# The second layer's bias in a mixture-of-experts kernel: from 39 TensorE products to additions on VectorE, with the order of the work written anew

## The chip, the core and the metric

The kernel runs on one core of one Trainium2 chip. The metric is the device time of one execution in microseconds (us), with the median of several runs.

## The reference, cut to what matters

The input is x, of 2 x 2048 rows of 128 numbers. Each row is normalised; the normalised rows go through causal attention and, beside it, through a layer of eight experts (each row uses one); both results are added to x.

```python
xn = _layernorm(x)
# attention, per batch of 2048 rows
scores = einsum('bsd,de,bte->bst', xn, qk, xn) / SCALE      # causal mask, softmax over t
attn_out = einsum('bst,btd,de->bse', attn, xn, ov)
# experts: D = 128, F = 512, E = 8
eid   = argmax(xn @ centroids.T)                            # one expert for each row
alpha = sigmoid(sum(xn * centroids[eid]))
xln   = layernorm(xn) * ln_g[eid] + ln_b[eid]
h     = relu(xln @ w1[eid] + b1[eid])
y     = h @ w2[eid] + b2[eid]                               # the bias of this page is b2
out   = x + attn_out + (xn + alpha * y)
```

## The kernel before, in words

All five engines take their work from one hand-written list, ORDER (lines 68 to 131). A word such as `OUT.7` is a job with its arguments. Each engine walks through the whole list and carries out the jobs that are its own, in the list's order; semaphores connect the engines. So the list sets the order on every queue, and a job that waits holds up all that stands behind it on its engine.

Precision is got by splitting a number into a 16-bit high half and a 16-bit low half (`_hi`, `_lo`), and multiplying high by high, high by low and low by high.

The work falls into stages. The names are those of the jobs.

- Start: rows are loaded and normalised (VAR, LE, RN, ROW on VectorE and ScalarE, XA on ScalarE), turned (T), projected (Q, V), and the first matrices of the experts are folded with gain and bias (W1, then W1h and W1l for their halves; for experts 4 to 7 the low half W1l is VectorE's). W2 and W2l split the second matrices.
- Attention, steps 0 to 51 of 80: `M` computes a block of scores only for its row maxima, `MR` (VectorE) reduces it, `RM` joins the maxima, `SH` turns them, `SHa` (ScalarE) writes them into row 0 of the queries as the shift. Then for each step `X` (TensorE, three products) computes scores, `EH` and `EX` (ScalarE) their exponentials, `XL` (VectorE) the low half, `P` and `PB` (TensorE) the weighted sums, and `QT` (VectorE) divides.
- Routing: CH, PL, BLK and SIG on VectorE find each row's expert and its place. `SC` (GpSimd, 32 indirect transfers) scatters the rows sorted by expert, each with its weight alpha/256 and its row number behind it, into `sorted_x`. SyncE then reads them back, turned for TensorE (`turn_rows`) and plain (`load_rows`, into `xs`, which is the tile `xn`).
- Experts: 39 tiles of 128 sorted rows. `HI.k` (lines 1434 to 1436, 12 products of 128 columns) computes the hidden layer of tile k, `RE.k` (ScalarE, line 1165) its high half with the relu, `LO.k` (VectorE, line 1014) its low half, and `OUT.k` (lines 1454 to 1460, 13 products) the output. Three hidden tiles may be on their way at once (HB = 3). TensorE's order runs `HI` two or three tiles ahead of `OUT`. The first of the 13 products, line 1454, adds the bias: the stationary operand is `pick`, a matrix of the expert's one-hot column, the moving operand the high and low halves of b2 (`b2_hl`). `REG` loads the list of experts into TensorE's registers, 20 words with two experts each, and every operand of an expert is addressed through them.
- `YS.k` (ScalarE, line 1173) evicts two tiles of output from PSUM, scaled by each row's weight, into `xs`. `SO.t` (GpSimd, line 679, 39 indirect transfers) stores tile t by row number into `sorted_y`; it waits for the eviction of its pair (`s_ysb`).
- End: the last 28 steps of attention (52 to 79) run on TensorE, while SyncE loads `sorted_y` back (line 566, eight transfers, after all stores) and `Y` (VectorE, line 933) adds it to x; the rows go out as they are finished.

Three preparations serve the bias alone: two small transfers of b2, its split on ScalarE (line 1092) and VectorE (line 958), and the building of `pick` on ScalarE (line 1095, job PICK).

Of the kernel before, what the change touches and what calls it, by code (L numbers as in the profile page):

```python
# [72 lines left out]
Z.3 W1.2 M.0.0.0.0 M.0.0.2.0 M.0.0.3.0 M.0.0.1.0 W1b.1 W1b.2 V.1 T.2 M.0.1.0.1 M.0.1.2.0 W1.3 M.0.1.1.1 M.0.1.3.1 W1b.3
M.0.1.0.0 SH.0.0 M.0.1.3.0 Tl.2 MR.0.1.0.1 MR.0.1.2.0 MR.0.1.1.1 MR.0.1.3.1 MR.0.1.0.0 ROW.4.6 ROW.6.8 MR.0.1.3.0 R2
MR.0.1.1.0 MR.0.1.2.1 W1l.4 W1l.5 RM.0.1 Ql.2 MR.0.2.0.1 MR.0.2.2.1 MR.0.2.2.0 MR.0.2.3.2 MR.0.2.0.2 MR.0.2.3.1 W1h.2
XA.2 W1l.1 Vf.1 Ta.2 W1l.2 LE.4.6 LE.6.8 W1h.3 W2.0 W2.1 W1l.3 SHa.0.0 XA.3 W1h.4 W1h.5 Qa.2 EX.0 XA.5 EX.1 EX.2 SHa.0.1
R2a W1.4 W1.5 M.0.1.1.0 M.0.1.2.1 Q.2 X.0 X.1 X.2 M.0.2.0.1 M.0.2.2.1 P.0 M.0.2.2.0 SH.0.1 M.0.2.3.2 M.0.2.0.2 M.0.2.3.1
# [1416 lines left out]
```

## Time and profile before

| what | us |
|---|---|
| median of 3 runs (213.14 to 215.27) | 214.18 |
| the profiled execution, its time | 215.02 |
| the profiled execution, its span | 213.3 |
| TensorE busy in the span | 201.8 |
| VectorE busy in the span | 172.8 |
| ScalarE busy in the span | 159.2 |

The span runs from the first to the last instruction; the 1.72 us by which the execution's own time is longer lie around it. Times in the rows are us from the span's start. A busy TensorE is not one at its peak: a product of 128 columns is shown as 0.22 us long, while the next one starts 0.056 us after it.

### The profile page before, as it was taken

The page shows a single profiled execution, that of the slowest core. Times are in us where ns is not written, and L with a number is a line of the kernel's source. Part 1 is how long each engine was busy: PE and PEld are TensorE (multiplying, and loading weights), DVE is VectorE, ACT ScalarE, POOL GpSimd, SP SyncE. Part 2 cuts the span into 40 slices and gives each one's busy share as a digit, 9 for nine tenths or more (in the row PEclk, how much of TensorE's full clock was granted, in tenths as well). Part 3 has the DMA queues.
Part 4 walks back from the last instruction along what each step waited for, and adds up shares of the span by engine and source line. Part 5 has one row for each costly group of instructions (what it writes and reads, how often), then busy time and mean ns, then how long its engine had stood idle before and what let it go on. Part 6 is the DMA issues. An engine that isn't in the chain of part 4 may idle for free.

```text
span 213.3 us, 6804 instructions
## 1 busy us (share of the span) xinstructions
PE 201.8 (95%) x2404; PEld 157.2 (74%) x2404; DVE 172.8 (81%) x449; ACT 159.2 (75%) x370; POOL 112.7 (53%) x159
## 2 busy tenths in 40 slices
PE   7887798999999999999979999999999999999993
PEld 5644256779677856777648999999999987777782
DVE  5899998989999999999999857549376564559974
ACT  2689996899978898787886664655765568988881
POOL 7338557972618787776760256676355677300000
PEclk9999999999999999999999999999999999999998
DMA  5993004168112111111117856665771111194065
GB/s 171 302 292 112 2 0 153 51 219 268 50 52 82 47 52 53 50 50 53 50 33 151 149 127 151 141 138 77 157 165 38 52 52 55 49 292 130 0 194 155
DMA packets 37616, 23.54 MB, mean 110 GB/s; under 512 B 12488, under 2 KB 34160, under 8 KB 37584
## 3 DMA queue, kind: packets, MB, share of 16 engines
q1 hardware_dynamic: 34976, 18.28, 33.5%
q0 software_dynamic: 2272, 4.69, 6.7%
q8 instruction: 20, 0.33, 0.7%
q10 hardware_dynamic: 336, 0.14, 0.3%
q14 instruction: 12, 0.10, 0.2%
HBM read 11.17 MB, written 9.38 MB: 96 GB/s over the span
## 4 chain that ended last, share of the span: by engine, by line
PE 79%; ACT 5%; DVE 2%; issue 2%; DVEq 0%; ACTq 0%
PE psum L1298 6%; PE psum L1299 6%; PE psum L1297 6%; PE psum L1350 6%; PE psum L1342 6%; PE psum L1343 6%; PE psum L1276 6%; PE psum L1434 4%; PE psum L1460 4%; PE psum L1436 4%; PE psum L1435 4%; PE psum L1458 4%; PE psum L1459 4%; PE psum L1333 4%; ACT xn L1063 1%
## 5 line engine op out<-in xcount | busy, mean ns | idle before, releaser
L679 POOL DMA_INDIRECT sorted_y<-xn x39 | 38.2, 980 | 26.8 <-ACT xn L1173 14.3
L896 DVE TENSOR_TENSOR p_lo<-p_sb,p_hi 128x512 f16<-128x512 f32 (+1 forms) x68 | 42.3, 654 | 11.1 <-ACT p_sb L1046 10.9
L1040 ACT ACTIVATE p_hi<-psum 128x512 f16<-128x512 f32 (+1 forms) x68 | 35.9, 545 | 15.8 <-PE psum L1350 12.6
L1014 DVE SCALAR_TENSOR_TENSOR h_lo<-psum,h_hi 128x512 f16<-128x512 f32 x39 | 26.6, 690 | 21.3 <-ACT h_hi L1165 21.1
L671 POOL DMA_INDIRECT sorted_x<-xr,pos x32 | 33.1, 1034 | 15.4 <-issue 10.2
L1046 ACT ACTIVATE p_sb<-psum 128x512 f32<-128x512 f32 (+1 forms) x80 | 39.4, 544 | 0.1
L1165 ACT ACTIVATE h_hi<-psum 128x512 f16<-128x512 f32 x39 | 23.2, 599 | 17.9 <-PE psum L1436 16.9
L882 DVE TENSOR_REDUCE row_max<-psum 128x1 f32<-128x512 f32 x48 | 31.6, 682 | 0.7 <-PE psum L1276 0.5
L1342 PE MATMUL psum<-v_hi,p_hi 128*128 128x129 f16 x236 | 31.2, 221 | 0.0
L1343 PE MATMUL psum<-v_lo,p_hi 128*128 128x128 f16 x236 | 31.2, 219 | 0.0
L1276 PE MATMUL psum<-kT_hi,qT_hi 128*128 128x512 f16 (+3 forms) x80 | 26.0, 349 | 4.9 <-DVE row_max L878 1.9
L1458 PE MATMUL psum<-w_hl,h_hi 128*128 x156 | 28.1, 219 | 0.0
L1459 PE MATMUL psum<-w_hl,h_hi 128*128 x156 | 28.1, 219 | 0.0
L1460 PE MATMUL psum<-w_hl,h_lo 128*128 x156 | 28.1, 219 | 0.0
L1297 PE MATMUL psum<-qT_hi,kT_hi 128*128 128x512 f16 (+1 forms) x80 | 27.8, 347 | 0.0
L1298 PE MATMUL psum<-qT_lo,kT_hi 128*128 128x512 f16 (+1 forms) x80 | 27.8, 347 | 0.0
L1299 PE MATMUL psum<-qT_hi,kT_lo 128*128 128x512 f16 (+1 forms) x80 | 27.8, 347 | 0.0
L1434 PE MATMUL psum<-x2T,w_hl 128*128 128x128 f16 x156 | 27.5, 219 | 0.1
L1435 PE MATMUL psum<-x2T,w_hl 128*128 128x128 f16 x156 | 27.5, 219 | 0.0
L1436 PE MATMUL psum<-x2T,w_hl 128*128 128x128 f16 x156 | 27.5, 219 | 0.0
L1342 PEld LDWEIGHTS psum<-v_hi,p_hi 128*128 128x128 f16 x236 | 23.0, 98 | 2.2 <-DVE x_sb L923 0.5
L1343 PEld LDWEIGHTS psum<-v_lo,p_hi 128*128 128x128 f16 x236 | 23.1, 98 | 1.7
(190 smaller groups left out, 493.5 us busy)
## 6 DMA issues: line engine op xcount, KB each, us to landing
w_raw<-in_L_ffn_w SPq DMA_DIRECT2D x16, 256.0 KB, 5.0
sorted_x<-zero SPq DMA_DIRECT2D x3, 780.0 KB, 4.7
xn<-sorted_x SPq DMA_DIRECT2D x8, 260.0 KB, 4.1
x_sb<-in_L_attn_input_data SPq DMA_DIRECT2D x8, 256.0 KB, 5.7
xn<-sorted_y SPq DMA_DIRECT2D x8, 256.0 KB, 5.0
out<-x_sb SPq DMA_DIRECT2D x6, 256.0 KB, 3.1
sorted_y<-xn POOLq DMA_INDIRECT x39, 2.9
sorted_x<-xr,pos POOLq DMA_INDIRECT x32, 2.5
```

The costliest lines, as they stand in the source:

```text
L679: pool.indirect_dma_start(out=sorted_y[:, :], out_offset=bass.IndirectOffsetOnAxis(ap=tokens, axis=0), in_=xs[:, t % SLOTS, 0:P], in_offse ...
L896: v.tensor_tensor(p_lo[:, u, off:GW], p_sb[:, u, off:GW], p_hi[:, u, off:GW], ALU.subtract).then_inc(s_plo, 1)
L1046: a.activation(p_sb[:, u, off:GW], bank[SCORE[n % R]][:, off:GW], ACT.Exp, scale=SCALE).then_inc(s_exp, 1)
L1276: mm(at[:, 0:w], qT_hi[:, q:q + P], kT_hi[:, k:k + w], start=True, stop=True).then_inc(s_mm, 1)
L1297: mm(at[:, off:GW], kT_hi[:, kk], qT_hi[:, q], start=True, stop=False)
L1298: mm(at[:, off:GW], kT_hi[:, kk], qT_lo[:, q], start=False, stop=False)
L1299: m = mm(at[:, off:GW], kT_lo[:, kk], qT_hi[:, q], start=False, stop=not diag)
L1342: mm(to[i], w, v_hi[:, kt, 0:P + 1], start=(j == 0 and (i % 2 == 0 or (i == GT - 1 and (b, g) == LAST_QT[:2]))), stop=False, skip_group_ch ...
L1343: mm(to[i][:, 0:P], w, v_lo[:, kt, :], start=False, stop=False, skip_group_check=True)
L1458: mm(to, h_hi[:, h, at], hi, start=False, stop=False, skip_group_check=True)
L1459: mm(to, h_hi[:, h, at], lo, start=False, stop=False, skip_group_check=True)
L1460: m = mm(to, h_lo[:, h, at], hi, start=False, stop=(c == FC - 1), skip_group_check=True)
```

## The change

The product of line 1454 is gone, with `pick`, `b2_hl` and their preparation; the first product of a tile's first chunk now starts the accumulation. In their place

- SyncE loads b2 broadcast to all 128 partitions (job `B2`, 128 x 1024 numbers) into `A_e`, which the first matrices no longer need then. It waits until all eight of them are done;
- ScalarE scales that by 256 (job `B2s`, one instruction, between YS.0 and RE.5);
- VectorE loads the list of experts into its own registers (`REGv`, between LO.4 and LO.5) and, after each eviction YS.k, adds bias times weight to the evicted tiles (`YB.k`, one SCALAR_TENSOR_TENSOR for each of the two tiles, 39 in all, the bias addressed by register);
- GpSimd's stores wait for YB (`s_yb`) in place of YS.

ORDER is written anew throughout: the jobs other than these are the same, in another sequence.

```diff
 ORDER = entries("""
-... RE.0 RE.1 RE.2 RE.3 YS.0 RE.4 RE.5 RE.6 YS.1 YS.2 RE.7 ...
+... RE.0 Qa.7 RE.1 RE.2 RE.3 RE.4 YS.0 B2s RE.5 RE.6 RE.7 YS.1 YS.2 ...
...
-    N_FILL = 6
+    N_FILL = 5
...
-        w1_bytes, w2_bytes, pick_bytes = (flat(t[:]).bitcast(U8) for t in (w1_hl, w2_hl, pick))
+        w1_bytes, w2_bytes = (flat(t[:]).bitcast(U8) for t in (w1_hl, w2_hl))
+        b2_all = A_e
+        b2_bytes = flat(b2_all[:]).bitcast(U8)
...
-            for dst, src in ((b1_sb[0:E, :], b1), (b1_sb[E:2 * E, :], b1),
-                             (b2_sb[0:E, :], b2), (b2_sb[E:2 * E, :], b2)):
+            for dst, src in ((b1_sb[0:E, :], b1), (b1_sb[E:2 * E, :], b1)):
...
+                if job[0] == "B2":
+                    sp.wait_ge(s_w1p, E)
+                    sp.dma_start(flat(b2_all[:]), bass.AP(b2.tensor, 0, [[0, P], [1, E * P]])).then_inc(s_b2, 16)
...
             def store_rows(t):
-                pool.wait_ge(s_ysb, t // FT + 1)
+                pool.wait_ge(s_yb, t // FT + 1)
...
+            def add_bias(k):
+                if k == 0:
+                    v.wait_ge(s_b2s, 1)
+                v.wait_ge(s_ysb, k + 1)
+                t = k * FT % SLOTS
+                for i in range(min(FT, NS - k * FT)):
+                    bias = b2_bytes[:, bass.ds(expert[k * FT + i] * (4 * P), 4 * P)].bitcast(F32)
+                    to = xs[:, t + i, 0:P]
+                    ins = v.scalar_tensor_tensor(out=to, in0=bias, scalar=xs[:, t + i, WEIGHT:TOKEN], in1=to,
+                                                 op0=ALU.mult, op1=ALU.add)
+                ins.then_inc(s_yb, 1)
...
-                if kind == "PICK":
-                    a.wait_ge(s_const, 3)
-                    a.activation(pick[:], choice[:].unsqueeze(2).broadcast_to([P, E, P]), ACT.Copy,
-                                 scale=W_SCALE).then_inc(s_pick, 1)
...
+                if kind == "B2s":
+                    a.wait_ge(s_b2, 16)
+                    a.activation(flat(b2_all[:]), flat(b2_all[:]), ACT.Copy, scale=W_SCALE * W_SCALE).then_inc(s_b2s, 1)
...
-                mm(to, biases, b2_hl[:], start=(t == 0), stop=False, skip_group_check=True)
                 for c in range(FC):
...
-                    mm(to, h_hi[:, h, at], hi, start=False, stop=False, skip_group_check=True)
+                    mm(to, h_hi[:, h, at], hi, start=(t == 0 and c == 0), stop=False, skip_group_check=True)
```

Three places in the queues show it. The first is TensorE at an output tile (OUT) behind the last product of a hidden tile. Before, the register rows of lines 1451 and 1453 and the bias product stand ahead of the twelve products of the second matrix:

```order
L1436 MATMUL psum<-x2T,w1_hl 128x128
L1451 ISA
L1453 ISA
L1454 MATMUL psum<-b2_hl,pick 128x128
L1458 MATMUL psum<-w2_hl,h_hi 128x128
L1459 MATMUL psum<-w2_hl,h_hi 128x128
L1460 MATMUL psum<-w2_hl,h_lo 128x128
```

After, at such a place:

```order
L1460 MATMUL psum<-x2T,w1_hl 128x128
L1474 ISA x2
L1478 MATMUL psum<-w2_hl,h_hi 128x128
L1479 MATMUL psum<-w2_hl,h_hi 128x128
L1480 MATMUL psum<-w2_hl,h_lo 128x128
```

One product of the thirteen is gone. The second place is VectorE in the middle of the experts. Before, the low halves of the hidden tiles (`h_lo`, LO) alternate with reductions of score blocks (`row_max` and the masked form, MR):

```order
L878 ISA masked,row_max<-psum,late_keys 128x256
L878 ISA row_max 128x1
L1014 SCALAR_TENSOR_TENSOR h_lo<-psum,h_hi 128x512 x5
L882 TENSOR_REDUCE row_max<-psum 128x1
L1014 SCALAR_TENSOR_TENSOR h_lo<-psum,h_hi 128x512 x5
```

After, from LO.10 to LO.11 (the tile `xn` is `xs`, `A_e` holds the biases):

```order
L1041 SCALAR_TENSOR_TENSOR h_lo<-psum,h_hi 128x512
L1030 REGISTER_ALU
L1030 ISA
L1030 SCALAR_TENSOR_TENSOR xn<-A_e,xn 128x128
L1030 ISA
L1030 SCALAR_TENSOR_TENSOR xn<-A_e,xn 128x128
L1030 REGISTER_ALU
L1030 ISA
L1030 SCALAR_TENSOR_TENSOR xn<-A_e,xn 128x128
L1030 ISA
L1030 SCALAR_TENSOR_TENSOR xn<-A_e,xn 128x128
L1041 SCALAR_TENSOR_TENSOR h_lo<-psum,h_hi 128x512
```

Two YB jobs stand together there, four additions with six register rows between one LO and the next; of the 17 YB jobs among the LO and MR jobs twelve stand in such twos. The third place is ScalarE at the end of the start, around SHa.0.1 (the second row of `qT_hi` 1x128). Before, three exponentials (`p_sb`, EX.0 to EX.2) stand ahead of it:

```order
L1063 ACTIVATE xn<-x_sb,mr,r 128x127 x4
L1123 ACTIVATE w_hl<-psum 128x512 x2
L1104 ACTIVATE qT_hi<-psum 128x512
L1046 ACTIVATE p_sb<-psum 128x512
L1063 ACTIVATE xn<-x_sb,mr,r 128x127 x4
L1046 ACTIVATE p_sb<-psum 128x384
L1046 ACTIVATE p_sb<-psum 128x256
L1140 ACTIVATE qT_hi<-psum 1x128 x4
```

After, they stand behind it, and one of the two `w_hl` of the first matrices (W1h.5) as well:

```order
L1089 ACTIVATE xn<-x_sb,mr,r 128x127 x4
L1125 ACTIVATE qT_hi<-psum 128x512
L1144 ACTIVATE w_hl<-psum 128x512
L1089 ACTIVATE xn<-x_sb,mr,r 128x127 x4
L1161 ACTIVATE qT_hi<-psum 1x128 x4
L1072 ACTIVATE p_sb<-psum 128x512
L1072 ACTIVATE p_sb<-psum 128x384
L1072 ACTIVATE p_sb<-psum 128x256
L1144 ACTIVATE w_hl<-psum 128x512
```

What step 3 of attention waits for, SHa.0.1, has moved ahead of four instructions.

## Rows read from the trace of the kernel before

**Rows 1.** The page: busy time, and TensorE and VectorE in 40 slices (tenths).

```profile
PE 201.8 (95%) x2404; PEld 157.2 (74%) x2404; DVE 172.8 (81%) x449; ACT 159.2 (75%) x370; POOL 112.7 (53%) x159
...
PE   7887798999999999999979999999999999999993
...
DVE  5899998989999999999999857549376564559974
```

**Rows 2.** Windows: stretch, length, busy PE, PEld, DVE, ACT, POOL, then clock, DMA share, GB/s.

```profile
0.00:33.40 33.40, 27.37 (x141) 14.91 (x142) 30.12 (x135) 26.77 (x75) 19.65 (x66) 1.00 0.49 140
33.40:107.00 73.60, 73.50 (x776) 54.26 (x775) 70.23 (x180) 61.56 (x138) 50.43 (x51) 1.00 0.27 89
107.00:118.60 11.60, 9.95 (x130) 7.92 (x129) 11.49 (x23) 8.11 (x18) 4.39 (x4) 1.00 0.50 108
118.60:176.50 57.90, 57.90 (x967) 54.79 (x965) 36.52 (x63) 35.14 (x83) 32.56 (x34) 1.00 0.51 110
```

**Rows 3.** Waits of TensorE: total us, times, longest; its first row.

```profile
PE psum L1276 <- DVE row_max L878: 1.9, 2, 1.5
```

**Rows 4.** Timeline of TensorE, one output tile: its bias product and the products after it.

```profile
121.89 0.22 PE L1454 MATMUL psum<-b_hl,pick 128*128 128x128 f16 x1
121.95 0.22 PE L1458 MATMUL psum<-w_hl,h_hi 128*128 x1
...
122.62 0.22 PE L1434 MATMUL psum<-x2T,w_hl 128*128 128x128 f16 x1
```

**Rows 5.** Groups by line: count, busy us, mean ns, idle before.

```profile
L1014 DVE SCALAR_TENSOR_TENSOR h_lo<-psum,h_hi 128x512 f16<-128x512 f32 x39 | 26.6, 690 | 21.3 <-ACT h_hi L1165 21.1
...
L923 DVE SCALAR_TENSOR_TENSOR x_sb<-psum,inv_den,x_sb 128x128 f32<-128x128 f32 x30 | 9.1, 347 | 0.5
L1454 PE MATMUL psum<-b_hl,pick 128*128 128x128 f16 x39 | 8.6, 220 | 0.0
...
L1095 ACT ACTIVATE pick<-choice 128x1024 f16<-128x1024 f32 x1 | 1.0, 1044 | 0.0
```

**Rows 6.** Timeline of VectorE: two additions of 128 columns in a row.

```profile
104.81 0.61 DVE L923 SCALAR_TENSOR_TENSOR x_sb<-psum,inv_den,x_sb 128x128 f32<-128x128 f32 x2
```

**Rows 7.** Waits of VectorE: the longest in total.

```profile
DVE h_lo L1014 <- ACT h_hi L1165: 21.1, 22, 1.9
```

**Rows 8.** The chain that ended last, from 107 to 112 us: start, us, what.

```profile
108.98 2.05 issue
111.02 0.68 DVE masked L878
111.77 0.39 PE psum L1276
```

**Rows 9.** Timeline of TensorE around REG, which stands between the two products of L1276.

```profile
91.65 0.70 PE L1276 MATMUL psum<-kT_hi,qT_hi 128*128 128x128 f16 x2
92.19 0.39 PE L1350 MATMUL psum<-v_hi,p_lo 128*128 128x129 f16 x4
```

**Rows 10.** Timelines at the end of the start: VectorE, ScalarE and TensorE.

```profile
28.55 1.29 DVE L978 SCALAR_TENSOR_TENSOR w_hl<-psum,w_hl 128x512 f16<-128x512 f32 x2
29.75 0.16 DVE L890 TENSOR_REDUCE max_col<-row_max 128x4 f16<-128x8 f32 x1
29.82 0.68 DVE L967 SCALAR_TENSOR_TENSOR qT_lo<-psum,qT_hi 128x512 f16<-128x512 f32 x1
...
32.01 1.09 ACT L1140 ACTIVATE qT_hi<-psum 1x128 f16<-1x128 f32 x4
...
33.16 0.39 PE L1276 MATMUL psum<-kT_hi,qT_hi 128*128 128x512 f16 x1 [0.58 <-ACT qT_hi L1140]
```

**Rows 11.** Timelines of GpSimd, SyncE and VectorE: last store, loads of sorted_y, first Y.

```profile
182.03 1.34 POOL L679 DMA_INDIRECT sorted_y<-xn  x1 [0.30 <-issue]
...
184.78 5.50 SPq L566 DMA_DIRECT2D xn<-sorted_y  x8
...
191.93 0.68 DVE L933 TENSOR_TENSOR x_sb<-x_sb,xn 128x512 f32<-128x512 f32 x1
```

More of the change, by code:

```diff
@@ L73 @@
[L73 to L77, printed above, removed]
@@ new lines @@
+YS.10 RE.24 RE.25 RE.26 YS.11 YS.12 RE.27 RE.28 RE.29 RE.30 YS.13 RE.31 RE.32 YS.14 YS.15 RE.33 RE.34 RE.35 YS.16 RE.36
+RE.37 RE.38 YS.17 QT.0.3.0 QT.0.3.1 XL.40 XL.41 XL.42 Sl.7 W1l.6 XL.43 QT.1.0.0 QT.1.0.1 MR.1.2.2.2 MR.1.2.3.0 W1l.7
+XL.44 XL.45 XL.46 MR.1.2.0.1 MR.1.2.3.2 MR.1.2.1.2 MR.1.2.1.0 XL.47 XL.48 XL.49 MR.1.2.0.2 MR.1.2.2.1 XL.50 XL.51
+QT.1.1.0 QT.1.1.1 LO.0 LO.1 Ql.7 LO.2 LO.3 LO.4 REGv LO.5 MR.1.2.1.1 LO.6 LO.7 LO.8 MR.1.2.2.0 LO.9 YB.0 RM.1.2 LO.10
+YB.1 YB.2 LO.11 MR.1.3.0.2 LO.12 LO.13 MR.1.3.3.3 LO.14 YB.3 YB.4 LO.15 MR.1.3.2.2 LO.16 LO.17 MR.1.3.2.0 LO.18 YB.5
@@ L206, in build @@
         choice = sb("choice", [P, E])
-        pick = sb("pick", [P, E, P], F16)
         pick_first = sb("pick_first", [P, E, P], F16)
@@ L354, in build @@
         s_alpha = sem("s_alpha")
+        s_b2 = sem("s_b2")
+        s_b2s = sem("s_b2s")
+        s_yb = sem("s_yb")
         s_index = sem("s_index")
@@ L886, in row_maxima @@
                 v.wait_ge(s_max, units_done(b, g))
-                v.wait_ge(s_fill, 4)
+                v.wait_ge(s_fill, 3)
                 wait(v, s_negT, nth[job])
@@ L953, in work @@
                 if kind == "BIAS":
-                    v.wait_ge(s_bhi, 2)
-                    v.wait_ge(s_fill, 3)
+                    v.wait_ge(s_bhi, 1)
+                    v.wait_ge(s_fill, 2)
                     v.scalar_tensor_tensor(out=b1_hl[0:2 * E, :], in0=b1_sb[:], scalar=W_SCALE, in1=b1_hi[:],
-                                           op0=ALU.mult, op1=ALU.subtract).then_inc(s_bhl, 1)
-                    v.scalar_tensor_tensor(out=b2_hl[0:2 * E, :], in0=b2_sb[:], scalar=W_SCALE, in1=b2_hi[:],
                                            op0=ALU.mult, op1=ALU.subtract).then_inc(s_bhl, 1)
@@ L1005, in work, with load_experts @@
                     add_rest(job[1])
+                if kind == "REGv":
+                    v.wait_ge(s_tile_e, 1)
+                    load_experts()
+                if kind == "YB":
+                    add_bias(job[1])
+            expert = []
+            def load_experts():
+                _, pairs = nc.values_load_multi_w_load_instructions(
+                    tile_e[0:1, 0:NP], engines=[mybir.EngineType.DVE], min_val=0, max_val=E * E - 1,
+                    skip_runtime_bounds_check_because="two counts of at most E - 1 experts")
+                for pair in pairs:
+                    expert.extend(e.with_bounds(min_val=0, max_val=E - 1) for e in (pair & (E - 1), pair >> (E.bit_length() - 1)))
+            def add_bias(k):
[9 more added lines that the diff above has]
+                ins.then_inc(s_yb, 1)
             def rows_low(g):
@@ L1449, in output @@
                 to = bank[OUTPUT[u]][:, t * P:(t + 1) * P]
-                (biases,), w = expert_tiles(pick_bytes, expert[k], 1), expert_tiles(w2_bytes, expert[k], 2 * FC)
-                pe.lower_ap(biases, for_matmul_weights=True)
+                w = expert_tiles(w2_bytes, expert[k], 2 * FC)
                 for ap in w:
                     pe.lower_ap(ap)
-                mm(to, biases, b2_hl[:], start=(t == 0), stop=False, skip_group_check=True)
                 for c in range(FC):
```

121 lines of the change are left out of this document (57 added, 64 removed).

## The prediction

> **What bounds the kernel now.** I read the page first: TensorE is busy for 95% of the span and VectorE for 81%, and the 40 slices show TensorE full from about the seventh slice to the last but one [rows 1]. A busy TensorE can be half empty, so I took the windows by stage next [rows 2]. The reader is to see three things in them. In the first 33.4 us TensorE is idle for 33.40 - 27.37 = 6.0 us while VectorE is nearly full. From 33.4 to 107 and from 118.6 to 176.5 (attention, then the experts) TensorE has no idle time worth naming, 73.50 of 73.60 and 57.90 of 57.90. In the short stretch between them 11.60 - 9.95 = 1.65 us are lost. The waits of TensorE say the same: the longest in total is 1.9 us for a row maximum, in two waits of which one took 1.5 us [rows 3], and no wait for a low half of the hidden layer is among them, though the experts' whole stage hangs on these. In the timeline the thirteen products of a tile follow each other at an even pace [rows 4]. So in the stage that the change touches TensorE's own work sets the time: a product less there is a product's time less at the end, as long as the engines that feed TensorE keep up.
>
> VectorE is the one to look at for that. In the experts' stage it is busy for 36.52 of 57.90 us [rows 2], and nearly all the rest is waiting for ScalarE's high halves, 21.1 us in 22 waits, 0.96 us on average and 1.9 us at most [rows 7].
>
> **The change, part by part.** The sum is made against the profiled execution (215.02 us, a span of 213.3 us and 1.72 us around it). That execution lies 0.84 us above the median of the runs, 214.18 us; what comes out is taken off the median.
>
> *The products.* 39 go. From the first product behind a bias product to the next tile there are twelve, from 121.95 to 122.62, so 0.056 us each, and the bias product takes as much (121.89 to 121.95) [rows 4]. Its shown length of 220 ns [rows 5] overlaps with its neighbours and is not what it costs. 39 x 0.056 = 2.2 us, and since TensorE has no idle time in this stage all of it leaves the path: -2.2. The register rows ahead of each go as well, at no visible price, for the pace of [rows 4] holds across them.
>
> *The additions.* 39 come onto VectorE, 34 of them (YB.0 to YB.16) between the LO jobs and five behind XL.53. An addition of this operation and shape takes 347 ns by itself [rows 5] and 0.61/2 = 0.305 us in a row [rows 6]; that one reads PSUM and the new one does not, and no row shows the new one with its register-addressed operand. The low end is 0.305, the high end the 690 ns of the four times wider h_lo [rows 5]; I take 0.35, the row of the same shape. 34 x 0.35 = 11.9 us then lie in a stage that shrinks to 57.9 - 2.2 = 55.7 us and already holds 36.5 us and one reduction that moves into it, about as long as an h_lo (0.69 us [rows 5]): 49.1 of 55.7. On the average they fit. One by one they don't all: two YB jobs together are 4 x 0.35 = 1.4 us against a mean wait of 0.96, so the LO behind them starts some 0.45 us late, at six places, 2.7 us in all. TensorE runs the hidden layers two to three tiles ahead, 0.67 us of products for each, and can take up most of that. I count +0.4, with 0 and +2.7 as ends. While a YB waits for its eviction, the LO and MR jobs behind it wait too; in the new list each YB stands at least one LO behind the ScalarE job that it needs, so I cost that wait at nothing.
>
> *The registers and the table of biases.* REGv stands in front of LO.5. The same load on TensorE shows between the two products of L1276: from 91.65 to 92.19 are 0.54 us, and products of 128 and 512 columns need 5 x 0.056 = 0.28, so 0.26 us were lost [rows 9]. VectorE may pay more, since TensorE can have begun its load ahead of time; the high end is 2.05 us, the longest time in which VectorE stood still for nothing that the profile shows [rows 8]. Scaling the table is one instruction of 128 x 1024 on ScalarE, as long as the building of `pick` that goes, 1.04 us [rows 5], ahead of RE.5; ScalarE is busy for 35.14 of 57.90 us [rows 2]. The table's transfer waits on SyncE for the last first matrix, in the attention stage, and is wanted only in the experts' stage; nothing of SyncE's stands behind it but the turning of rows, which waits for GpSimd's scatter anyway. Together +0.15, from 0 to +2. The two transfers of b2, its split and `pick` stood where other engines set the pace: 0.
>
> The Trainium skill (Runtime: NRT & Kernel Launch, Instruction fetch mechanics) gives a register load about 200 ns for each register. For 20 words that would be 4 us on VectorE, an estimate by that page, where [rows 9] show 0.26 us on TensorE; it makes the third rival below.
>
> *The start.* What TensorE waits for last there is the shift of the second group: its block at 33.16 was held up 0.58 us by ScalarE [rows 10]. That hangs on RM.0.1, on VectorE at 29.75, behind two halves of first matrices that fill 28.55 to 29.75, 1.20 us [rows 10]. In the new list these two stand behind RM.0.1, as do the two short instructions of the second normalisation's R2 (I take 0.1 us for them, less than one max_col), and a qT_lo of 0.68 us stands ahead of it; on ScalarE the exponentials and a first matrix no longer stand ahead of the shift. So the shift can come 1.20 + 0.1 - 0.68 = 0.6 us sooner, and with it the point from which TensorE is full: -0.6. Of the 6.0 us of idle time a quarter is as much as I would credit (-1.5); the other end is that some job moved forward now waits, as long as the four copies of a shift take, +1.1 [rows 10].
>
> *The stall at 109.* VectorE stands still for 2.05 us there, waiting for nothing that the profile shows, and TensorE with it [rows 8]; that is nearly the whole 1.65 us lost in the stretch. Up to this place VectorE's queue is only two instructions shorter than before, so I leave it: 0, with -1.5 (gone or covered) and +1.5 (a second one among the experts) as ends.
>
> *The end.* GpSimd's stores now begin behind YB.0, which stands after LO.9, so five LO jobs later than YS.0 would let them. Before, the last store ended at 183.37, SyncE issued the loads from 184.78 on, and the first Y ran at 191.93 [rows 11]. The new list puts that Y two XL jobs later. I count 0, with +1 as the far end.
>
> Sum: -2.2 + 0.4 + 0.15 - 0.6 = -2.25 us. The profiled execution would come to 212.8 us, the median to 214.18 - 2.25 = 211.9 us.
>
> **The rivals.** *VectorE becomes the bound of the experts' stage* (slower). The place is the six double YB jobs, the price what an addition costs with its register row. For it: the stage is 88% full on VectorE by my own figure, and TensorE needs every low half soon after it is made. Against it: in attention TensorE ran full beside a VectorE at 70.23 of 73.60 us, 95% [rows 2]. The stage's slack of 55.7 - 37.2 = 18.5 us is used up at 18.5/34 = 0.54 us for an addition; from there each further 0.1 us costs 3.4 us. At the far end, 0.69, the stage is 34 x 0.15 = 5.1 us longer than TensorE's work, and with the 0.4 of my sum replaced by that the time is 211.9 - 0.4 + 5.1 = 216.6 us, 1.1% above before. At 0.6 us and the same way of counting it is 213.5 us.
>
> *The rewritten start gives nothing or loses.* For it: VectorE is full there, 30.12 of 33.40 us [rows 2], and a list that moves one job forward moves another back. Against it: the two halves did stand ahead of RM.0.1. Without the gain, and with 0.4 us lost, the time is 211.9 + 0.6 + 0.4 = 212.9 us.
>
> *The register load holds VectorE for microseconds.* With 4 us at LO.5, of which a wait of 0.96 us covers a part, TensorE loses about 3 us once: 211.9 - 0.15 + 3 = 214.8 us. Against it stands the 0.26 us of TensorE's load.
>
> *The stall at 109 vanishes too*: 211.9 - 1.5 = 210.4 us.
>
> **How the numbers follow.** About 1% is what a measurement of this kernel can tell from no change, so faster means below 212.0 us and slower above 216.3. My forecast has 0.53, its own range 210.9 to 212.9; it lies near the border, so I give 0.39 of that to faster and 0.14 to within. The vanished stall has 0.08, faster. VectorE as the bound has 0.20, half of it (0.10) slower. The start has 0.12 and the register load 0.07, within 1%, but for 0.02 of the latter where both go wrong. Faster 0.39 + 0.08 = 0.47; slower 0.12; within 0.41. The range of 8 in 10 goes from 210.2 to 215.2.
>
> **What would show it.** Right: no L1454 product, and a gap-free TensorE in the experts' stage that is some 2 us shorter; additions of about 0.3 to 0.35 us; VectorE's waits for h_hi down from 21 to 8 us or so; the first 33 us with less idle time of TensorE. Wrong: waits of TensorE for h_lo of more than a microsecond in total, a hole of VectorE in front of LO.5, waits for `sorted_y` in front of Y, or a TensorE that is idle for longer before 33 us than it was.

## The result and the profile after

The change makes the kernel slower: 223.84 us (median of 4 runs, 221.93 to 225.05) against 214.13 us, a ratio of 1.046 with a 95% interval of 1.042 to 1.050. The forecast was 211.9 us with a range of 210.2 to 215.2. The profiled execution took 223.4 us, its span 221.7 us in place of 213.3.

The page of the changed kernel, the rows that answer to [rows 1], with those of the granted clock:

```profile
PE 202.7 (91%) x2365; PEld 157.5 (71%) x2365; DVE 186.0 (84%) x486; ACT 158.2 (71%) x369; POOL 115.8 (52%) x159
...
PE   7599989999999699979969999999999999992993
...
DVE  5799999989999999998999758888878794435884
...
PEclk9759999999999999999999999999999999998898
```

Before, TensorE was full from about the seventh slice on but for one dent, at slice 23. Now there are dents at slices 14, 18, 21 and 37, and the clock falls near the start and near the end. The windows, with the columns of [rows 2], say how much each stage lost; the last row is of the kernel before, whose span ends there:

```profile
0.00:33.40 33.40, 28.07 (x134) 15.96 (x135) 28.89 (x128) 25.16 (x69) 20.19 (x66) 0.90 0.50 140
33.40:107.00 73.60, 70.16 (x761) 52.61 (x761) 70.67 (x172) 59.70 (x136) 47.92 (x48) 1.00 0.27 87
107.00:118.60 11.60, 9.65 (x91) 6.29 (x90) 11.19 (x23) 7.19 (x16) 6.41 (x6) 1.00 0.26 77
118.60:176.50 57.90, 57.65 (x969) 54.79 (x967) 46.25 (x104) 37.28 (x88) 27.68 (x29) 1.00 0.61 121
176.50:213.30 36.80, 32.71 (x354) 23.87 (x353) 23.85 (x49) 25.33 (x55) 13.61 (x12) 0.95 0.37 108
...
176.50:213.30 36.80, 33.05 (x398) 25.29 (x396) 24.43 (x49) 27.62 (x60) 5.65 (x5) 0.98 0.45 127
```

The experts' stage is nearly as full as it was, with VectorE busy for 46.25 us instead of 36.52. The attention in front of it and the end behind it are what has holes: 73.60 - 70.16 = 3.4 us where there was 0.1, and 36.80 - 32.71 = 4.1 us. Before, the last stretch has 3.75 us without a product too, but there it holds the tail of the span, which the changed kernel still has in front of it. The products of TensorE that waited longest show the places:

```profile
8.27 0.38 PE L1390 MATMUL psum<-CT,qk_sb 128*128 128x128 f32 x1 [1.95 <-DMA ov_sb<-in_L_attn_ov]
...
77.55 0.23 PE L1374 MATMUL psum<-v_hi,p_lo 128*128 128x129 f16 x1 [2.11 <-DVE p_lo L899]
98.12 0.32 PE L1321 MATMUL psum<-qT_hi,kT_hi 128*128 128x384 f16 x1 [1.28 <-ACT p_sb L1072]
116.53 0.28 PE L1300 MATMUL psum<-kT_hi,qT_hi 128*128 128x256 f16 x1 [1.95 <-DVE row_max L885]
203.49 0.61 PE L1374 MATMUL psum<-v_hi,p_lo 128*128 128x129 f16 x4 [4.09 <-DVE p_lo L899]
```

The wait at 116.53 is the hole of [rows 3, 8], the others are new. The span, 8.4 us longer, is cut where the first product of HI.0 and the last of OUT.38 start, before and after:

```profile
117.17 0.23 PE L1434 MATMUL psum<-x2T,w_hl 128*128 128x128 f16 x1
...
177.22 0.22 PE L1460 MATMUL psum<-w_hl,h_lo 128*128 x1
```

```profile
121.52 0.23 PE L1458 MATMUL psum<-x2T,w_hl 128*128 128x128 f16 x1 [0.20 <-issue]
...
179.88 0.22 PE L1480 MATMUL psum<-w_hl,h_lo 128*128 x1
```

The first hidden tile starts at 121.52 us instead of 117.17 (+4.35), the experts' stage takes 58.36 us instead of 60.05 (-1.69), and from its end to the end of the span there are 41.8 us instead of 36.1 (+5.7).

The last part is read from the end backwards. GpSimd's stores, SyncE's loads of `sorted_y` and the first additions of the loaded rows on VectorE, which answer to [rows 11]:

```profile
136.31 0.98 POOL L682 DMA_INDIRECT sorted_y<-xn  x1 [12.88 <-DVE xn L1030]
...
182.11 1.61 POOL L682 DMA_INDIRECT sorted_y<-xn  x1 [0.30 <-DVE xn L1030]
...
193.76 0.96 POOL L682 DMA_INDIRECT sorted_y<-xn  x1 [0.31 <-issue]
...
196.13 6.05 SPq L569 DMA_DIRECT2D xn<-sorted_y  x8
...
199.73 0.69 DVE L936 TENSOR_TENSOR x_sb<-x_sb,xn 128x512 f32<-128x512 f32 x1 [2.90 <-DMA xn<-sorted_y]
202.14 0.69 DVE L936 TENSOR_TENSOR x_sb<-x_sb,xn 128x512 f32<-128x512 f32 x1 [1.72 <-DMA xn<-sorted_y]
```

The last store begins 11.7 us later than before, the loads 11.3 us later. VectorE, which comes to Y at the place that the list gives it, stands there for the loaded rows, the low halves behind Y are late, and TensorE waits 4.09 us at 203.49. The stores are late because the additions are: YB.0 runs at 135.43, 7.1 us after the eviction YS.0 has ended, and YB.15 at 178.57, 9.5 us after YS.15. A store takes GpSimd 0.96 + 0.30 us, so 39 of them from 136.31 on cannot be done before 185.2, and each wait in between comes on top.

The second new reading is VectorE at the two holes of row maxima and weights, beside GpSimd:

```profile
73.67 3.82 DVE L899 TENSOR_TENSOR p_lo<-p_sb,p_hi 128x384 f16<-128x384 f32 x3
...
111.51 4.37 DVE L899 TENSOR_TENSOR p_lo<-p_sb,p_hi 128x512 f16<-128x512 f32 x3
```

```profile
75.06 2.27 POOL L723 TENSOR_TENSOR w_hl<-w_raw,w_hl 128x512 f16<-128x512 f32 x2
...
113.05 2.26 POOL L723 TENSOR_TENSOR w_hl<-w_raw,w_hl 128x512 f16<-128x512 f32 x2
```

The second hole has the same two rows in the kernel before:

```profile
106.72 4.38 DVE L896 TENSOR_TENSOR p_lo<-p_sb,p_hi 128x512 f16<-128x512 f32 x3
...
108.27 2.27 POOL L720 TENSOR_TENSOR w_hl<-w_raw,w_hl 128x512 f16<-128x512 f32 x2
```

Three of VectorE's subtractions take 1.9 us elsewhere when they are 512 columns wide, and 1.08 us when they are 384 and less, as the three at 73.67 are. Here they last 2.5 to 2.7 us longer, somewhat more than the 2.27 us of GpSimd's two subtractions (W2l.3 and W2l.4, then W2l.5 and W2l.6) that run into them. Both engines read two operands from SBUF. What [rows 8] call "issue", and the prediction took for a standstill of VectorE's own, was a wait for GpSimd that the profile doesn't name (e4 and e5 below show it). Before, W2l.2 to W2l.4 ran at 55.25 and 65.77, beside quotients and row maxima, which read PSUM; the new list has moved 3 and 4 behind the eighth transfer of the scatter.

One execution each of e3, e4 and e7 below was of a slower state of the chip and is left out of their ratios, though not of their medians; in e4 and e7 it is the profiled one, 2.5 us above the median, so only single rows of these two are used.

### The profile page after: what moved, and what is told of

It reads as the page before. It is cut to its first block, busy times and chain, and to the rows that moved or that the text cites. A ratio compares the mean times of both kernels' runs of the same rounds, so it can differ in the third digit from the quotient of the medians.

```text
span 221.7 us, 6821 instructions
## 1 busy us (share of the span) xinstructions
PE 202.7 (91%) x2365; PEld 157.5 (71%) x2365; DVE 186.0 (84%) x486; ACT 158.2 (71%) x369; POOL 115.8 (52%) x159
## 4 chain that ended last, share of the span: by engine, by line
PE 53%; DVE 16%; issue 10%; DMA 9%; ACT 8%; POOL 1%; DVEq 1%; ACTq 1%; SPq 0%; POOLq 0%
DVE p_lo L899 5%; DMA sorted_y<-xn 5%; PE psum L1458 4%; PE psum L1460 4%; PE psum L1459 4%; PE psum L1478 4%; DVE row_max L885 4%; PE psum L1480 4%; PE psum L1479 4%; PE psum L1300 4%; PE psum L1321 3%; PE psum L1374 3%; PE psum L1322 3%; PE psum L1323 3%; PE psum L1366 3%
## 5 line engine op out<-in xcount | busy, mean ns | idle before, releaser
L682 POOL DMA_INDIRECT sorted_y<-xn x39 | 40.1, 1029 | 31.2 <-DVE xn L1030 16.5
L899 DVE TENSOR_TENSOR p_lo<-p_sb,p_hi 128x512 f16<-128x512 f32 (+1 forms) x68 | 44.7, 693 | 8.7 <-ACT p_sb L1072 8.5
L674 POOL DMA_INDIRECT sorted_x<-xr,pos x32 | 33.6, 1050 | 20.0 <-issue 11.1
L1366 PE MATMUL psum<-v_hi,p_hi 128*128 128x129 f16 x236 | 32.2, 224 | 0.0
L1367 PE MATMUL psum<-v_lo,p_hi 128*128 128x128 f16 x236 | 32.1, 223 | 0.0
L1374 PE MATMUL psum<-v_hi,p_lo 128*128 128x129 f16 x236 | 22.1, 222 | 6.6 <-DVE p_lo L899 6.6
L1478 PE MATMUL psum<-w_hl,h_hi 128*128 x156 | 27.8, 219 | 0.1
L1479 PE MATMUL psum<-w_hl,h_hi 128*128 x156 | 27.7, 219 | 0.0
L1300 PE MATMUL psum<-kT_hi,qT_hi 128*128 128x512 f16 (+3 forms) x80 | 25.0, 349 | 3.0 <-DVE row_max L885 2.5
L1366 PEld LDWEIGHTS psum<-v_hi,p_hi 128*128 128x128 f16 x236 | 23.5, 100 | 1.9
```

Source lines behind the costliest of these rows:

```text
L682: pool.indirect_dma_start(out=sorted_y[:, :], out_offset=bass.IndirectOffsetOnAxis(ap=tokens, axis=0), in_=xs[:, t % SLOTS, 0:P], in_offse ...
L899: v.tensor_tensor(p_lo[:, u, off:GW], p_sb[:, u, off:GW], p_hi[:, u, off:GW], ALU.subtract).then_inc(s_plo, 1)
L1366: mm(to[i], w, v_hi[:, kt, 0:P + 1], start=(j == 0 and (i % 2 == 0 or (i == GT - 1 and (b, g) == LAST_QT[:2]))), stop=False, skip_group_ch ...
L1478: mm(to, h_hi[:, h, at], hi, start=(t == 0 and c == 0), stop=False, skip_group_check=True)
L1479: mm(to, h_hi[:, h, at], lo, start=False, stop=False, skip_group_check=True)
```

## The experiments

Theory A: the new list loses the time, by late stores and by holes ahead of the experts. Theory B: the additions and their registers lose it. The table has the medians, the kernel before measured beside each, and the three parts of the profiled execution's span as above, without those of e4 and e7. The ratios are of means, the intervals at 95%.

| run | median us | before us | ratio (95%) | to HI.0 | experts | after them |
|---|---|---|---|---|---|---|
| before | | | | 117.2 | 60.05 | 36.1 |
| after | 223.84 | 214.13 | 1.046 (1.042 to 1.050) | 121.5 | 58.36 | 41.8 |
| e1 | 221.28 | 213.31 | 1.035 (1.028 to 1.042) | 124.0 | 60.40 | 36.0 |
| e2 | 216.85 | 213.31 | 1.014 (1.009 to 1.019) | 117.2 | 61.10 | 36.4 |
| e3 | 219.08 | 213.31 | 1.021 (1.013 to 1.029) | 121.5 | 59.46 | 35.9 |
| e4 | 220.09 | 213.31 | 1.027 (1.019 to 1.035) | | | |
| e5 | 213.09 | 213.34 | 0.996 (0.993 to 0.998) | 115.8 | 60.06 | 36.0 |
| e6 | 211.77 | 213.34 | 0.991 (0.987 to 0.995) | 115.1 | 58.26 | 36.1 |
| e7 | 214.18 | 213.34 | 1.001 (0.997 to 1.005) | | | |
| e8 | 215.47 | 213.34 | 1.010 (1.007 to 1.014) | 118.5 | 59.52 | 36.0 |
| e9 | 213.82 | 213.21 | 1.002 (1.000 to 1.005) | 115.1 | 59.78 | 36.4 |
| e10 | 212.72 | 213.21 | 0.997 (0.994 to 0.999) | 115.5 | 60.59 | 36.6 |
| e11 | 217.28 | 213.21 | 1.018 (1.015 to 1.021) | 117.7 | 61.78 | 36.0 |
| e12 | 216.99 | 213.21 | 1.016 (1.014 to 1.019) | 118.4 | 61.26 | 36.0 |
| e13 | 212.69 | 213.30 | 0.995 (0.992 to 0.998) | 114.9 | 59.29 | 36.5 |
| e14 | 211.90 | 213.30 | 0.992 (0.990 to 0.995) | 115.0 | 58.35 | 36.4 |

**e1, the order alone.** The kernel before with the new list, less B2, B2s, REGv and YB, and with PICK behind EX.9.

```diff
-VAR.0.1 VAR.1.2 LE.0.1 LE.1.2 C1a C0a BIASa C2a AE.0 Ta.0 AE.1 AE.2 AE.3 Ta.1
+VAR.0.1 VAR.1.2 LE.0.1 LE.1.2 BIASa C0a C1a C2a AE.0 Ta.0 Ta.1 LE.2.3 AE.1 AE.2
...
```

> The kernel before (bias products on TensorE) with the list of the changed kernel, less its four new jobs. Theory A (the time is lost by the order: stores of the experts' rows that wait for late additions, and three holes before the experts): the first store comes right behind the first eviction again, so the hole at the end goes, and the holes before the experts stay: first hidden tile near 121.5 us, time 217 to 219 us. Theory B (the additions themselves and their registers cost the time): as before, 213 to 215 us.

The new list costs 3.5% without a single addition, more than theory A had put down, and all of it ahead of the experts: HI.0 is 6.8 us late, the rest as before. The stores start behind the first eviction again and the hole at the end is gone. Theory B cannot be the main cause.

Not all of the 6.8 us are holes. Behind two of them the granted clock fell (third column from the end):

```profile
76.00:84.00 8.00, 7.26 (x51) 4.43 (x52) 6.99 (x18) 4.72 (x9) 5.32 (x6) 0.79 0.32 100
...
117.00:125.00 8.00, 7.48 (x80) 6.29 (x81) 5.76 (x17) 3.67 (x10) 0.33 (x1) 0.79 0.79 161
```

With TensorE busy nearly all the time there, that is some 2 x 8 x 0.21 = 3 us, an estimate from these rows.

**e2, the additions in the old order.** The changed kernel's code with the list of before, each YB right behind a low half.

```diff
-X.47 W1.7 M.1.2.1.0
+X.47 W1.7 B2 M.1.2.1.0
...
-RE.3 YS.0 RE.4
+RE.3 YS.0 B2s RE.4
...
-LO.3 Ql.7 RM.1.2 LO.4 LO.5
+LO.3 REGv Ql.7 RM.1.2 LO.4 YB.0 LO.5
...
```

> The changed kernel's arithmetic in the list of the kernel before, each pair of additions right behind the first low half after its eviction. Theory A: experts' stage 1.7 to 2.2 us shorter, last store near 183 us, time 211.5 to 213 us. Theory B: 220 us or more, with waits of TensorE for low halves or a hole behind the register load.

A miss on both sides: 216.85 us. HI.0 and the end are as before, but the experts' stage is 61.10 us, longer than with the bias products. Eight times TensorE starts a product only 0.34 to 0.55 us after the one before it there; with no bias at all (e6) that happens once. The reading is that an addition directly behind a low half pushes back the next low half, and TensorE with it, so that the place of an addition has a price. e7 tests it.

**e3, early additions in the new order.** YB.0 to YB.17 right behind the first low half after their eviction.

```diff
-LO.5 MR.1.2.1.1 LO.6 LO.7 LO.8 MR.1.2.2.0 LO.9 YB.0 RM.1.2
+LO.5 YB.0 MR.1.2.1.1 LO.6 LO.7
...
```

> The changed kernel with YB.0 to YB.17 moved forward in its list, each right behind the first low half after its eviction. Theory A: first store near 131.5 us in place of 136.3, last store near 185 us in place of 194, VectorE's waits for the loaded rows and TensorE's hole of 4.25 us near the end gone: 217.5 to 219.5 us. Theory B: 223 to 225 us as it is.

```profile
131.37 0.98 POOL L682 DMA_INDIRECT sorted_y<-xn  x1 [7.94 <-DVE xn L1030]
...
186.23 0.95 POOL L682 DMA_INDIRECT sorted_y<-xn  x1 [0.30 <-issue]
```

Of this kernel's stores, on GpSimd, the first is 4.9 us and the last 7.5 us sooner than after the change. The part behind the experts falls from 41.8 to 35.9 us; it is as short as before, so the late stores were the whole of that loss. The stage gives back 1.1 us; the additions stand right behind low halves again, as in e2.

**e4, GpSimd's halves ahead of the scatter.**

```diff
-W2l.2 SC.0
+W2l.2 W2l.3 W2l.4 SC.0
...
-SC.7 W2l.3 W2l.4 SC.8
+SC.7 SC.8
```

> The changed kernel with GpSimd's low halves of the second matrices 3 and 4 ahead of the scatter, where GpSimd has 7 us free. Theory A (GpSimd's subtraction of two SBUF operands holds up VectorE's subtraction of two SBUF operands): the three low halves of weights at 73.7 take 1.9 us in place of 3.8, TensorE's hole of 2.28 us at 77.5 is gone, time 1 to 2.5 us less than the changed kernel, 221.5 to 223. Rival (VectorE stands still there for its own program): the stretch of 3.8 us stays, 223 to 225 us.

```profile
52.70 3.39 POOL L723 TENSOR_TENSOR w_hl<-w_raw,w_hl 128x512 f16<-128x512 f32 x3
...
54.08 0.92 DVE L838 TENSOR_SCALAR tiles_f<-tiles_f 128x8 f32<-128x8 f32 x1
55.03 1.08 DVE L839 TENSOR_SCALAR tiles_f<-tiles_f 128x8 f32<-128x8 f32 x1
...
74.12 1.08 DVE L899 TENSOR_TENSOR p_lo<-p_sb,p_hi 128x384 f16<-128x384 f32 x3
```

The hole at 77.5 is gone; the three low halves that stood beside GpSimd there now take 1.08 us. GpSimd's three subtractions now run from 52.70 to 56.1. VectorE's routing is held up there: two operations on 128 x 8 numbers, 0.15 to 0.2 us each otherwise, last 0.92 and 1.08 us, though they read one operand each from SBUF and not two; the next low half is late, and TensorE waits 0.58 us at 59.07. The holding up moves with GpSimd's jobs, which a cause inside VectorE's program would not do. The time, 220.09 us, is lower than the 221.5 to 223 expected.

**e5, the kernel before with one wait on GpSimd.**

```diff
                     pool.wait_ge(s_w2hi, e + 1)
+                    if e == 5:
+                        pool.wait_ge(s_plo, 35)
```

> The kernel before with one wait more: GpSimd begins the low half of the second matrix 5 only when VectorE has finished the low half of the weights of step 46. Theory A (two engines that both read two SBUF operands hold each other up): the three low halves of weights at 106.7 take 1.9 us in place of 4.38, TensorE's hole of 1.70 us at 111.8 is gone or under 0.4, time 211.3 to 212.3 where the kernel before has 213.3. Rival (VectorE's own stand-still there, as the prediction took it): the 4.38 us stay, time as before.

```profile
107.24 1.90 DVE L898 TENSOR_TENSOR p_lo<-p_sb,p_hi 128x512 f16<-128x512 f32 x3
```

```profile
109.27 2.27 POOL L722 TENSOR_TENSOR w_hl<-w_raw,w_hl 128x512 f16<-128x512 f32 x2 [0.51 <-ACT w_hl L1135]
```

VectorE's three low halves take 1.90 us where they took 4.38 before, and TensorE's hole is gone: the standstill of [rows 8] is explained. The time falls by 0.4% (0.2 to 0.7), less than the 1.7 us of the hole. The runs say why. The 31 executions of the kernel before beside this one fall into two groups, 17 between 212.8 and 213.9 and 14 between 214.1 and 215.5; the ten of this kernel lie between 212.7 and 214.0. The hole is there in some executions only: the profiled execution of before (215.02 us) was one with it, while e6 and e9 have none in theirs without any such wait. In these two GpSimd begins W2l.5 at 109.2, when the three low halves are done.

**e6, no bias at all.** The 39 products are left out of the kernel before, and nothing adds b2.

```diff
-                mm(to, biases, b2_hl[:], start=(t == 0), stop=False, skip_group_check=True)
...
-                    mm(to, h_hi[:, h, at], hi, start=False, stop=False, skip_group_check=True)
+                    mm(to, h_hi[:, h, at], hi, start=(t == 0 and c == 0), stop=False, skip_group_check=True)
```

> The kernel before without the 39 bias products and with nothing in their place; its output lacks b2. If a product is worth 0.056 us in a full TensorE: experts' stage 60.05 - 2.2 = 57.9 us, time 2.0 to 2.4 us below the kernel before. Rival (the stage is set by the exchange between TensorE, ScalarE and VectorE, and the shorter tile only waits longer): stage 59 to 60 us, time less than 1 us below.

The stage is 1.79 us shorter, somewhat less than the 2.2 expected, and the time 0.9% (0.5 to 1.3). This is what the products cost, and the most that moving the bias can bring. The ten executions again fall into two groups, five between 211.05 and 211.36 and five between 212.17 and 213.13: nothing here keeps the hole of e5 away.

**e7, the additions in VectorE's waits.** The old list, each YB in front of a low half for which VectorE had waited.

```diff
-LO.4 LO.5 LO.6 LO.7
+LO.4 REGv LO.5 YB.0 LO.6 YB.1 YB.2 LO.7
...
```

> The additions in the list of the kernel before, as in the run before, but each in front of a low half for which VectorE waited for ScalarE there. Theory A (an addition costs by its place: right behind a low half it pushes the next one back, in a wait it is free): experts' stage 58 to 59 us in place of 61.1, TensorE's small holes there under 1 us in total, time 212 to 214. Theory B (VectorE is too full for 39 additions whatever their place): stage 60.5 us or more, time 216 to 217.5 as in the run before.

214.18 us against 216.85 for the same additions behind the low halves: the place is worth 2.7 us, as theory A said, though the time is just above its 214. But nothing is gained yet over the kernel before.

**e8, early additions and GpSimd's halves apart.** e3 with W2l.3 ahead of SC.0, W2l.4 behind SC.1, and the wait of e5 for step 49.

```diff
-W2l.2 SC.0 SC.1 SC.2
+W2l.2 W2l.3 SC.0 SC.1 W2l.4 SC.2
...
+                    if e == 5:
+                        pool.wait_ge(s_plo, 38)
```

> The early additions in the new list, and GpSimd's low halves of second matrices moved: 3 ahead of the scatter, 4 behind its second transfer, 5 behind the low half of the weights of step 49. Theory A: TensorE's holes of 2.3 us at 76 and 2.1 us at 115 go, the first hidden tile comes near 117.5 us in place of 121.5, time 214 to 216 us where the early additions alone had 219.1. Rival: the holes stay or come back at the next step, 218 us or more.

```profile
118.52 0.23 PE L1460 MATMUL psum<-x2T,w_hl 128*128 128x128 f16 x1 [0.92 <-DMA x2T<-sorted_x]
```

The two holes go, HI.0 comes 3.0 us sooner than in e3 and the time falls by some 3 us to 215.47. A smaller hole of 1.05 us comes at 66.7, where W2l.4 now meets one low half (2.08 us instead of 0.69). At 118.52 TensorE now waits for turned rows. The scatter's last transfer was issued by 111.43, and the turning began only at 115.16, 3.7 us later; before it was 110.46 - 108.24 = 2.2 us. The change's table of biases, 512 KB, is in flight there: SyncE issues it at 108.57 us and it lands at 113.16.

**e9, the two small transfers of b2 again.** e7 with these lines back, into a tile that nothing reads.

```diff
+            for dst in (b2_sb[0:E, :], b2_sb[E:2 * E, :]):
+                sp.dma_start(dst, b2).then_inc(s_b2x, 16)
```

> The run with the additions in VectorE's waits, and the two small transfers of b2 that the change took out of the start issued again (into a tile that nothing reads). Theory A (they kept the first large transfers of first matrices back by 0.7 us, behind the two matrices qk and ov): ov lands 3.5 to 3.8 us after its issue in place of 5.4, the first products of C1 start before 7.0 us in place of 7.9, no stretch at half clock in the first 20 us, time 212.5 to 213.5 where it was 214.2. Rival (ov is late by chance): ov takes 4.5 us or more, time as it was.

The DMA rows of `ov_sb` (size, median us from issue to landing), after the change and in this run:

```profile
ov_sb<-in_L_attn_ov ACTq DMA_DIRECT2D x1, 64.0 KB, 5.7
```

```profile
ov_sb<-in_L_attn_ov ACTq DMA_DIRECT2D x1, 64.0 KB, 3.8
```

Without the two transfers SyncE issues the four large loads of first matrices at 2.67 us instead of 3.34; `ov` is issued at 2.49. Over all the profiles, ov took 4.4 to 5.7 us in kernels without the two transfers and 3.5 to 4.2 us in those with them. C1 starts at 6.82 us here (7.91 in e7), the clock stays at 1.00. The median moved little, from 214.18 to 213.82 us, which is within what the two runs leave open: the late `ov` is shown, its worth in time is not. The waits also show the register load on VectorE:

```profile
122.54 0.69 DVE L1046 SCALAR_TENSOR_TENSOR h_lo<-psum,h_hi 128x512 f16<-128x512 f32 x1 [0.76 <-ACT h_hi L1194]
124.21 0.69 DVE L1046 SCALAR_TENSOR_TENSOR h_lo<-psum,h_hi 128x512 f16<-128x512 f32 x1 [0.98 <-issue]
```

Between LO.4 and LO.5 stands only REGv: 0.98 us, after which TensorE waited 0.72 us for this low half.

**e10, the old order mended.** e9 with the wait of e5, and the table of biases loaded behind the second tile's rows.

```diff
                 turn_rows(pairs)
                 load_rows(pairs)
+                if pairs == LOADS[1]:
+                    sp.wait_ge(s_w1p, E)
+                    sp.dma_start(flat(b2_all[:]), bass.AP(b2.tensor, 0, [[0, P], [1, E * P]])).then_inc(s_b2, 16)
```

> The same with two more edits: GpSimd's wait for the low half of the weights of step 46 ahead of second matrix 5, and the table of biases loaded behind the second tile's rows instead of ahead of the first. If the three losses are apart from each other, the bias on VectorE now gains what the shorter experts' stage gives, about 1 us: 211.5 to 212.5 us, no execution near 215. Rival: 213 us or more, the additions give back what the products take.

212.72 us, a little under before, and a smaller gain than forecast. The parts in the table are those of its slowest execution, 214.49 us. The wait for turned rows did not go, it went to the next tile: 1.19 us at 122.18.

**e11, the table later in the new order.** e8 with the edit of e10.

```diff
-                if job[0] == "B2":
...
+                if pairs == LOADS[1]:
...
```

> The new list with early additions and GpSimd's halves moved, and the table of biases loaded behind the second tile's rows. Theory A (the 512 KB of the table delay the rows of the first tiles): turned rows begin 2.2 to 2.6 us after the scatter's end in place of 3.7, TensorE's hole of 1.07 us at 118.5 for x2T is gone, time 0.7 to 1.2 us below the 215.5 of that run. Rival (the scatter's own end sets it): the hole stays, 215 to 216 us.

Wrong: 217.28 us, 1.8 us more than e8. The turning did begin 2.4 us after the scatter's end (113.69), as theory A said, and the first wait for x2T became small, but one of 1.59 us at 124.92 took its place. The table delays the rows that it stands among, wherever that is.

**e12, three edits in the new order.** e11 with the transfers of e9 and a change at the hole of 96.5 us.

```diff
-X.35 PB.31 PB.32
+PB.31 X.35 PB.32
...
-X.38 X.39 PB.34 M.1.2.3.1 PB.35 M.1.2.0.0
+X.38 M.1.2.3.1 M.1.2.0.0 X.39 PB.34 PB.35
```

> The run with the table later, with the two small transfers of b2 back at the start, and at the hole of 1.4 us at 96.5 the product PB.31 ahead of X.35 and the two blocks of M.1.2 ahead of X.39. If the hole is a matter of TensorE's list there: under 0.6 us, and C1 before 7 us; time 213 to 214 us, about the kernel before. Rival (ScalarE is simply too late there): the hole of 1.2 us or more stays, 214 to 215 us.

The hole stays (1.21 us at 96.84), so it isn't a matter of where these jobs of TensorE stand, and the time, 216.99 us, misses both forecasts. The hole comes in every run of the new list and in none of the old. The rival on record, that ScalarE is late there, fits the changed kernel's trace: the product waits for an exponential (`p_sb`), and ScalarE runs from 94.89 to 97.94 without a gap behind the copies of a shift (1.09 us at 93.39). Which of the moved jobs makes it so is open.

**e13, the table early.** e9 with the wait of e5, and the table in a tile of its own, loaded in the scatter's stage.

```diff
-        b2_all = A_e
+        b2_all = sb("b2_all", [P, E, P])
...
-                    sp.wait_ge(s_w1p, E)
...
-SC.1 W2l.4 SC.2
+SC.1 W2l.4 B2 SC.2
```

> The old list with the additions in VectorE's waits, the two small transfers and GpSimd's wait, and the table of biases in a tile of its own, loaded in the scatter's stage instead of among the experts' rows. Theory A (the table's 512 KB cost 1.2 us because they land among the turned rows): turned rows 1.4 to 2.4 us after the scatter's end, no hole for x2T above 0.4 us, experts' stage 59.0 to 59.5 us in place of 60.6, time 211.3 to 212.2. Rival: the hole stays somewhere, 212.7 us as in the run before.

**e14, and the register load one low half earlier.**

```diff
-RM.1.2 LO.4 REGv LO.5 YB.0
+RM.1.2 REGv LO.4 LO.5 YB.0
```

> The same with REGv one low half earlier, in front of LO.4, where VectorE waits 0.75 us anyway. If VectorE's register load takes about 1 us (0.98 us in front of LO.5 in the run with the small transfers): the hole of 0.8 to 0.9 us for h_lo at the fourth output tile falls below 0.4, time 0.3 to 0.6 us below the run beside it. Rival: the hole moves with it, same time.

In e13 the waits for turned rows are gone and the stage is 59.29 us, as expected, though the median stays at 212.69, above the 211.3 to 212.2 expected; one hole of 0.72 us for a low half, behind REGv, is left. In e14 it is gone too:

```profile
121.91 1.29 DVE L1047 SCALAR_TENSOR_TENSOR h_lo<-psum,h_hi 128x512 f16<-128x512 f32 x2 [0.76 <-ACT h_hi L1195]
123.12 0.61 DVE L1036 SCALAR_TENSOR_TENSOR xn<-b_all,xn 128x128 f32<-128x128 f32 x2
```

LO.4 and LO.5 follow each other, and REGv lies in the wait of 0.76 us ahead of them. e14 takes 211.90 us, 0.8% (0.5 to 1.0) under the kernel before; it beats both kernels. Its stage is 58.35 us, against 58.26 without any bias (e6). Part of the gain is GpSimd's wait, worth 0.4% by itself (e5); the median of e14 lies 1.2 us under that of e5. That it is also close to e6's (211.77) flatters it, since e6 has no such wait; the spans of the two profiled executions, both without the hole, are 209.8 and 209.4 us.

## Why the prediction was wrong, by its own steps

- *The products* and *the additions* had the right mechanism, and their sum was right partly by luck. Forecast -2.2 + 0.4; leaving the products out brings -1.8 in the stage (e6), and the additions cost 0.1 us in the right places (e14), 2.8 in the wrong ones (e2). The two errors cancel. An addition takes 0.345 us, two together 0.60, as the rows of the same shape had said:

```profile
L1030 DVE SCALAR_TENSOR_TENSOR xn<-A_e,xn x39: 340/345/400, 135.4 to 181.9; 128x128 f32<-128x128 f32 x39
```

- The experts' stage of the changed kernel fell by 1.69 us where the sum had -2.2 + 0.4 + 0.15 = -1.65. VectorE's waits for high halves fell from the 21.1 us of [rows 7] to 9.4, near the 8 that were forecast:

```profile
DVE h_lo L1041 <- ACT h_hi L1189: 9.4, 13, 1.5
```

  The rival *VectorE becomes the bound* fails at its own point: 0.345 us an addition, not 0.54.
- *The registers and the table*: the register load took 0.98 us on VectorE, inside the bounds, nearly four times the 0.26 of the low one and half the 2.05 of the high one. In the changed kernel it lay in a wait of 1.32 us ahead of LO.5 and cost nothing; the old list had to make room for it (e14). "Nothing of SyncE's stands behind it but the turning of rows" was the wrong half of this step: the turning is what the table delays, and TensorE waited 0.92 to 1.59 us for the rows (e8, e10, e11). In the changed kernel itself no such wait shows; HI.0 starts there 4.8 us after the turning begins (3.4 in e8). The third rival's 4 us did not come. The Trainium skill (Runtime: NRT & Kernel Launch, Instruction fetch mechanics) gives about 200 ns for a register, with HBM as the source in its list of terms; this load reads `tile_e` in SBUF. The measured 0.98 us for 20 words is a quarter of the 4 us that the prediction estimated from that figure.
- *The end* is the first step that failed. It was counted at 0, with +1 as the far end, from five LO jobs between YS.0 and YB.0. It cost 5.7 us (e3), and the prediction's own sign for it came, waits for `sorted_y` in front of Y. The mistake was looking at the first addition alone: the stores are a queue of 1.26 us each, so their end hangs on when they begin and on every late addition behind, and YB.15 and YB.16 stand behind the last low half and three row maxima.
- *The start* failed as a boundary. That the new list brings the point at which TensorE is full forward by some 0.6 us was half right at most: X.0, at 27.82 us before, came 0.5 to 0.9 us sooner in e1, e3 and e8, but it came 0.3 to 0.4 sooner in e9, e13 and e14 with the old list too, and 0.65 us later in the changed kernel's profile. There the late `ov` held TensorE for 1.95 us and the clock fell to 0.7 and 0.5 in the second and third slice. TensorE is busy for longer in the first 33.4 us, 28.07 us instead of 27.37, which was to be a sign of being right; at the lower clock (0.90 on the mean) it is none. "The two transfers of b2 ... stood where other engines set the pace: 0" is the sentence that fell: the 0.67 us that they held SyncE had kept large loads out of the way. What that costs in time is open (e9).
- *The stall at 109* was costed at 0, and it stayed. But its cause was read wrongly, as VectorE's own, and so the same could not be seen coming at 74. The sum had no term for the attention stage at all, though the list was new there, and this is the second step that failed: 4.35 us until HI.0. The rows add up to about that: 0.65 for the later X.0, 2.11 for the new hole at 77.5, 1.28 for the one at 98, and 0.4 by which the hole at 116.5 outlasts the 1.53 us of before. With the two meetings of GpSimd's and VectorE's subtractions out of the way HI.0 came 3.0 us sooner (e3 against e8). A look at GpSimd's queue in the two lists would have shown W2l.3 and W2l.4 moved. The Trainium skill (SBUF — State Buffer, Who interferes with whom) has the rule: a VectorE instruction with two SBUF inputs contends with a GpSimd instruction that reads SBUF, and the one that comes second waits for the whole of the other. The trace agrees, 4.37 us against 1.90.
- The prediction gave *slower* 0.12, nearly all for VectorE as the bound of the experts' stage. What made the kernel slower, the end and the attention stage, none of its rivals named.

## What to carry to other kernels

A list that is written anew is a change of its own, and it has to be costed stage by stage on every queue, GpSimd's and SyncE's too; here it cost 3.5% by itself, while the arithmetic, with its places mended, was worth 0.8% the other way, about half of it by GpSimd's wait. Work put on an engine that has idle time is free only in its waits: with the register load and the table, the same 39 additions cost the stage 2.8 us in e2 and 0.1 us in e14, against no bias at all (e6). Where the profile shows an engine busy for twice an operation's usual time, or "issue" in a chain, look at what the other engines did in the same microseconds; here it was GpSimd beside VectorE.
